# Feed-forward stage of a one-layer language model tower: the order of up-products, down-products and the last sum

## The reference

```
x = x + fused                                            # residual after the attentions
h2 = _ln(x, norm_mlp_w, norm_mlp_b)                      # layer norm, 128 features
x = x + (gelu(h2 @ mlp_w1.T + mlp_b1) @ mlp_w2.T + mlp_b2)   # 128 -> 512 -> 128
...
h = h + _L0_ffn_ref(...)                                 # outer residual
```

## Time and profile before

| | us |
|---|---|
| median of 3 runs | 1671.6 (1670.5 to 1672.09) |
| the profiled execution's own time | 1672.9 |
| its span | 1671.1 |
| PE busy over the span | 1517.6 (91%) |
| DVE / ACT / POOL busy | 1245.2 / 1106.5 / 1020.2 |

### The profile page before, as it was taken

How to read it: one execution, slowest core, us unless ns; L and a number is a source line. 1 busy time by engine, 2 the same in 40 slices (tenths; PEclk the granted TensorE clock), 3 DMA queues, 4 the chain that set the end, 5 groups by cost and what they waited for, 6 DMA issues and landing times. The chain is left out here.

```text
span 1671.1 us, 37358 instructions
## 1 busy us (share of the span) xinstructions
PE 1517.6 (91%) x8662; PEld 661.0 (40%) x8662; DVE 1245.2 (75%) x3454; ACT 1106.5 (66%) x2137; POOL 1020.2 (61%) x1375
## 2 busy tenths in 40 slices
PE   3657976889999999999999999999999999875998
PEld 1215962233333333333333334333333333212665
DVE  6885866578887988888798888879788888353442
ACT  3333760647878788787877878787787878823333
POOL 6841435466686777767677777767767775523443
PEclk9867976889999999999999999999999999957999
DMA  1321118355554565456456546545655654121221
GB/s 48 77 52 30 45 32 110 49 77 74 75 84 66 72 78 83 64 77 82 64 75 78 79 63 80 79 63 79 78 76 62 86 70 50 15 25 33 64 63 57
DMA packets 134645, 109.27 MB, mean 65 GB/s; under 512 B 24128, under 2 KB 127552, under 8 KB 134592
## 3 DMA queue, kind: packets, MB, share of 16 engines
q1 hardware_dynamic: 132544, 104.45, 42.8%
q0 software_dynamic: 2048, 4.20, 1.0%
HBM read 19.26 MB, written 8.39 MB: 17 GB/s over the span
## 5 line engine op out<-in xcount | busy, mean ns | idle before, releaser
L1122 ACT ACTIVATE probs<-psum 128x512 f32<-128x512 f32 (+3 forms) x1536 | 755.7, 548 | 226.4 <-PE psum L1237 215.6
L1022 DVE TENSOR_REDUCE mx_S<-psum 128x1 f32<-128x512 f32 x512 | 326.3, 681 | 47.9 <-PE psum L1217 47.3
L1022 DVE TENSOR_REDUCE mx_C<-psum 128x1 f32<-128x512 f32 x512 | 318.0, 677 | 45.2 <-PE psum L1217 45.2
L1018 DVE CUSTOM_DVE_ANT_0 psum<-psum,causal 128x128 f32<-128x128 f32 (+3 forms) x512 | 243.3, 509 | 98.0 <-PE psum L1217 95.4
L1217 PE MATMUL psum<-ks_S,qs_S 96*128 96x512 bf16 x512 | 196.8, 395 | 10.8 <-DMA ks_S<-parts_k 6.1
L1217 PE MATMUL psum<-ks_C,qs_C 96*128 96x512 bf16 x512 | 199.7, 398 | 4.5 <-DMA ks_C<-parts_k 1.3
L1237 PE MATMUL psum<-qs_C,ks_C 99*128 99x512 bf16 x512 | 189.3, 385 | 3.6 <-ACT probs L1122 3.2
L1237 PE MATMUL psum<-qs_S,ks_S 99*128 99x512 bf16 x512 | 191.2, 385 | 0.2
L903 POOL CAST parts_q<-f_q 128x512 bf16<-128x512 f32 x48 | 29.3, 611 | 226.2 <-ACT f_q L1113 225.7
L1217 PE MATMUL psum<-ks_T,qs_T 96*128 96x128 bf16 (+3 forms) x512 | 156.1, 307 | 1.6 <-DVE mx_S L1022 1.0
L1237 PE MATMUL psum<-qs_T,ks_T 99*128 99x256 bf16 (+3 forms) x512 | 152.5, 302 | 2.8 <-ACT probs L1122 1.5
(11 more groups left out here) (182 smaller groups left out, 2720.2 us busy)
## 6 DMA issues: line engine op xcount, KB each, us to landing
qs_S<-parts_q SPq DMA_DIRECT2D x96, 128.0 KB, 4.4
ks_S<-parts_k SPq DMA_DIRECT2D x96, 128.0 KB, 4.8
qs_T<-parts_q SPq DMA_DIRECT2D x96, 128.0 KB, 4.4
ks_T<-parts_k SPq DMA_DIRECT2D x96, 128.0 KB, 4.6
qs_C<-parts_q SPq DMA_DIRECT2D x96, 128.0 KB, 4.3
ks_C<-parts_k SPq DMA_DIRECT2D x96, 128.0 KB, 5.0
w_in_S<-in_s_in SPq DMA_DIRECT2D x16, 257.0 KB, 2.8
w_in_T<-in_t_in SPq DMA_DIRECT2D x16, 257.0 KB, 2.7
```

The source lines that it names most:

```text
L1018: nc.vector.tensor_tensor_reduce(tile[:, 0:last_key], tile[:, 0:last_key], causal[:, T - last_key:T], 1.0, NEG, ALU.add, ALU.max, mx[kind] ...
L1022: nc.vector.tensor_reduce(mx[kind][:, n:n + 1], tile, AX_X, ALU.max, negate=True).then_inc(reduced, 1)
L1122: nc.scalar.activation(probs[:, group_place(kind, b, n // 4), n % 4, t0:T], psum[:, LOGITS + ring_place(kind, b, n, RC), t0:T], ACT.Exp, s ...
```

## The change

On PE, up(i - 2) moves ahead of down(i - 3) in each step. On DVE, finish moves one step back: step i does finish(i - 4) in place of finish(i - 3). No function's body, no buffer and no other engine's program changes.

```diff
@@ DVE stages @@
                     if exists(b - 1):
                         scale_shift(b - 1, 1 - odd)
-                    if exists(b - 3):
-                        finish(b - 3, 1 - odd)
+                    if exists(b - 4):
+                        finish(b - 4, odd)
@@ PE stages @@
                 def stages(b, odd):
                     if exists(b):
                         turn(b, odd)
+                    if exists(b - 2):
+                        up(b - 2, odd)
                     if exists(b - 3):
                         down(b - 3, 1 - odd)
-                    if exists(b - 2):
-                        up(b - 2, odd)
```

## The result

The changed kernel takes 1660.75 us (median of 6 runs, 1659.1 to 1661.67) against 1671.84 (6 runs, 1670.5 to 1673.21): a ratio of 0.9933, with an interval of 0.9920 to 0.9946. It is 11.1 us faster. I had forecast a gain of 9.4 us and a time of 1662.2. The sign and the mechanism came out as forecast.

A forecast was written before the change was run, and what follows sets the result against it. TensorE bounds the kernel, idle mainly in waits for each batch's last GELU. The profiled 1672.9 us less 9.4 of waits is 1663.5; runs' median lies 1.3 lower, so 1662.2, range 1660.7 to 1665.6.

The forecast's parts named there:

- What bounds the kernel: TensorE, busy 77.09 of 80.88 us over ten batches, its idle mostly waits for the last GELU ahead of the down-products.
- TensorE's order, the sum: Stretch from turn(3) to the last downs, 125.92 us: ups 51.45, downs 59.04, turns 5.98, leaving waits of 9.4 to go.
- a down behind an up: TensorE's new neighbours without a wait, not in the trace: priced at 0, bounds 0 to 0.07 us a batch.
- The beginning: Stage's start: up(1) at about 1542.2, everything ahead of 1541.72 stays, down(0) some 3 us later at no harm.
- VectorE's order: Last sum one step back keeps VectorE off the path: slack 3.8 us at the turn, 1.8 over the round, cost 0.
- GpSimd at the end: `base` before the last sum takes 3.36 us plus about 0.1 handing over, fitting within 3.68 with 0.2 to spare.
- Only the recorded idle goes: Rival: a turn still costs its recorded 0.60, 1.8 us come back, 1664.0 to 1664.4; 16% together with a branch remnant.
- Register work and branch: Rival: TensorE's register instructions and loop branch show, 7.2 us, 1669.4 (4%); or a branch remnant of 0.6 to 2.4.
- VectorE and GpSimd shut each other out: Rival: `base` beside the normalisation bars VectorE's work, round 7.8 to 8.5 us, some 1674; 2% slower, 1% in between.
- The clock: Rival: TensorE at half speed for 18 us of the stage gives back all 9.4; 2%, shared with anything unseen.
- The signs: Profile signs: `gT` wait under 0.3 us, down to down 7.5 to 7.65, turn to up 0.42 to 0.49, ScalarE's waits down some 9.

The follow-up runs named there:

- split-wait kernel: Kernel before with both orders untouched, the wait ahead of the down-products split over the first four products; ratio 0.9934 to the kernel before.
- wait put back: Changed kernel whose down-products also wait for the GELUs of the batch just multiplied up; ratio 1.0039 to the kernel before.
- order-alone kernel: Kernel before with TensorE's new order, VectorE's last sum left at step i - 3; ratio 1.0132 to the kernel before, 1.32% slower.

## Why the prediction was right in kind and short in size

**What bounds the kernel.** Right. Taking out nothing but the wait for the last GELU, by the order or by splitting the wait, gives the whole gain. Putting it back takes all of it away, and 4.6 us more, since no turn lies inside the wait there.

**TensorE's order, the sum.** The step that failed is the price of the down-products: "Down: 1578.62 - 1574.94 = 3.68 [...] 15 x 3.68 + 3.84 = 59.04". That price was read off downs that start at a wait. Such a down pays for its first weight load in the open, because the load stands behind the same wait. The weight loads of a down in the kernel before, and of one after:

```profile
1574.94 3.65 PEld L1497 LDWEIGHTS psum<-w,gT 128*128 128x128 f32 x32 [0.58 <-ACT gT L1469]
```

```profile
1544.73 0.19 PEld L1497 LDWEIGHTS psum<-w,gT 128*128 128x128 f32 x1 [0.24 <-issue]
1545.16 3.54 PEld L1497 LDWEIGHTS psum<-w,gT 128*128 128x128 f32 x31 [0.24 <-issue]
```

Before, the first load starts with the first pass, at 1574.94. After, it starts 0.43 us ahead of it, while the last up-product runs. The first pass then has 272 to 275 ns; behind a wait it has 377, which the line view of the kernel before shows as its maximum, and which I had not looked at:

```profile
L1497 PE MATMUL psum<-w,gT x315: 275/275/377, 1559.8 to 1640.0; 128*128 128x128 f32 x158
```

The down behind the one late turn lies between the two, and TensorE had not been idle just before it:

```profile
1639.64 3.65 PEld L1497 LDWEIGHTS psum<-w,gT 128*128 128x128 f32 x32
```

```profile
L1497 PE MATMUL psum<-w,gT x32: 275/275/309, 1639.7 to 1643.2; 128*128 128x128 f32 x32
```

Its first load starts 0.07 us ahead of its first pass at 1639.71, and that pass is 0.07 shorter, 309 ns. In the split-wait kernel the down behind the late turn has its load 0.11 ahead (1634.78 and 1634.89), and its first pass has 275. So it is the start of the load, and not idle time, that sets the first pass. A down without a wait takes 3.57. The stretch after is 13 turns of 0.44 (5.7, forecast 5.98), 15 ups of 3.43 to 3.44 (51.5, forecast 51.45) and 15 downs of 3.57 with one of 3.73 (57.3, forecast 59.04). So of the 1.9 us that the stretch is shorter than the 116.5 of my sum, 1.7 are the downs' and 0.3 the turns'. The wait put back shows it from the other side: the downs go back to 3.67, beside 0.97 a batch of bare wait.

My bounds were wrong with it. I gave "a down behind an up" 0 to 0.07 of extra cost, and no gain. But the earlier trace rows had the one down that had nothing to wait for, at 1643.32 - 1639.71 = 3.61, and I used that pair only to price the turn, with the 3.68 put in for the down. By that row the ends should have run from -0.07 a batch, and by the 377 ns from -0.10.

**The beginning.** Right: in this profile turn(3) starts 0.4 earlier, as the end of the attentions does, and up(1) follows 0.44 behind it at 1541.73.

**VectorE's order.** Right, and shown from both sides. `xs` takes 3.1 us in every batch of the loop. The round, from the start of the sum to the end of scale_shift, takes some 5.6 of 7.44, and TensorE never waits for it in the stretch; without the collision nothing changes. What I said of the sum left at i - 3 holds too, but its price was more than the 1.8 us a batch on VectorE: in four of the batches TensorE's granted clock also fell.

**GpSimd at the end.** Right, and closer than computed. The tail of the timeline:

```profile
1652.27 0.69 DVE L1436 TENSOR_TENSOR y<-base,psum 128x512 f32<-128x512 f32 x1 [6.32 <-PE psum L1497]
...
1654.36 1.27 POOL L1406 TENSOR_TENSOR base<-base,b 128x512 f32<-128x512 f32 x1
1655.84 0.69 DVE L1436 TENSOR_TENSOR y<-base,psum 128x512 f32<-128x512 f32 x1 [2.89 <-PE psum L1497]
```

`base` is done at 1655.63, 3.36 behind the start of the sum before it, and the last sum starts at 1655.84. Less the 0.1 of handing over that I had allowed, 0.1 was to spare, where I had computed 0.2 with a down of 3.68.

**The rivals.** *Only the recorded idle goes*: out, and in the wrong direction; the turn costs 0.44. The true gain was 4 us above what the waits name as idle. *Register work and branch*: none of it shows; the chain has no issue pieces within the loop or at its edges. *VectorE and GpSimd shut each other out*: the normalisation collides with `base`; scale_shift goes on beside GpSimd's root as before (0.78 us at 1553.75, the root's two instructions at 1553.91 and 1554.19). The statistics start at 1552.56, when `base` is done, so whether they would collide isn't shown. *The clock*: 1.00 in the whole stretch.

**The signs.** ScalarE's waits were to shrink by some 9 and shrank by 13.9 (94.4 to 80.5). That is the time by which its last GELU moved (1663.06 to 1648.70, less the 0.4 of the profile's earlier start); two downs now stand behind it, not one. The period was to be 7.5 to 7.65 and is 7.44.

## What to carry to other kernels

Price work that will lose its wait from instances that have none. The instance behind a wait carries its own start-up, here 0.10 us of a weight load in the open, beside the idle time that the profile names. Of two steps of a pipeline moved together, ask which one brings the gain and which only keeps the engine behind it off the path. And where an order is rewritten to cover a wait of 0.8 us, a split of the wait over its first readers may cover as much with no reordering.

## What the runs showed of the hardware that I had not expected

- A down that starts at a wait: first pass 377 ns instead of 275, the whole 3.68 instead of 3.57 us to the next. With its first weight load 0.07 us ahead the first pass had 309 ns, with 0.11 ahead 275, with 0.43 ahead 272.
- Waits of 1.8 to 3.8 us in every batch cost more than themselves: in four of the 12 batches of the order-alone kernel the up-products ran partly at half clock (4.5 to 5.5 us for 3.44), about 8 us in all with their turns. Waits of 0.94 to 1.02 us in every batch, in the kernel with the wait put back, left the granted clock at 1.00.
- 34 transposes of a unit matrix at the stage's start, with 8 of data among them, were followed by a granted clock of 1.00 before up(0), which otherwise began at 0.5.
- Four normalisation instructions beside two instructions of GpSimd took 3.07 to 3.10 us instead of 1.11.
